# First attention of a four-layer kernel: the sum of queries and maxima moves from VectorE to TensorE and ScalarE

## The chip, the cores and the metric

One Trainium2 chip, one of its cores. The metric is the device time of the whole kernel in microseconds, smaller is better. TensorE (PE) multiplies, VectorE (DVE), ScalarE (ACT) and GpSimd (POOL) do the rest, and SyncE (SP) issues the transfers. PEld is the loading of TensorE's stationary operand, which overlaps its matmuls.

## The reference

Four layers follow one another: a cross attention with mean and deviation over 256 channels (the first attention, L0), and then three more attentions with their dense layers and MLPs (L1, L2, L3). The change is within L0 alone. There x and ctx have shape (8, 128, 256): 8 sequences, 128 channels, 256 positions; 16 heads of 8 channels each.

```python
q = jnp.einsum('oc,bct->bot', Wq, x) + bq[None, :, None]
k = jnp.einsum('oc,bct->bot', Wk, kv) + bk[None, :, None]
v = jnp.einsum('oc,bct->bot', Wv, kv) + bv[None, :, None]
...
attn = jnp.einsum('bhqd,bhdk->bhqk', q * scale, k)
attn = jnp.where(kv_mask[:, :, None, :], attn, -jnp.inf)
attn = jax.nn.softmax(attn, axis=-1)
mean = jnp.einsum('bhqk,bhkd->bhqd', attn, v)
ex2 = jnp.einsum('bhqk,bhkd->bhqd', attn, v * v)
std = jnp.sqrt(jax.nn.relu(ex2 - mean * mean))
...
out = (xn * std + mean) * mask.astype(x.dtype)
```

## The kernel before, in words

L0 is cut into 32 steps, four for each of the 8 sequences; a step handles four heads, and it has 4 units of work. The order in which all this is issued is written out by hand in `l0_order`: a list of ticks, one for each unit, to which every other piece is pinned. Every engine walks the same list and does its own share, so each engine works strictly in that order. `S` is the score matmul of a unit, `X` is its second score matmul, which is followed by the exponential.

One step s passes through these pieces:

- `pp` (tick 4s-7). TensorE picks the four heads out of the dense queries and keys with selection matrices (`sel`), which are the stationary operand: two matmuls of 256 columns for the queries (L895), two for the keys (L897) and one for the key mask (L898), all into one bank of PSUM. Queries and keys come as two parts each (`dqk`, a rounded value and the remainder), which is why there are two of each. ScalarE copies the bank to `qk` (L1183), adding a one in a row of each head through the bias `ones0`. SP then moves the keys into a block form (`kbd`) with four DMAs.
- `S` (ticks 4s to 4s+3). One matmul of 512 columns (L913) gives scores with queries down the partitions, into one of three banks. VectorE reduces each to the negated maximum of every row (L1552).
- `NL` (tick 4s+4). GpSimd writes those maxima into `NM` as a rounded part and a remainder (L1665, L1666).
- `P2` (tick 4s+6). TensorE transposes `NM` with two matmuls of 128 columns (L905) into a general bank, and VectorE adds the bank to the queries in `qk` and writes `qs2` (L1559). `qs2` thus holds the queries and, in rows of their own, the maxima to be subtracted.
- `X` (unit u at tick u+9, so the first of the step comes at tick 4s+9). Two matmuls of 256 columns (L922), keys stationary and `qs2` moving, give the scores with keys down the partitions, less the maximum; two banks. ScalarE takes the exponential of 128x512 into `pt` (L1188).
- `PV` (every second step, tick 4s+14 for odd s). 16 matmuls with 32-column weights, shown as 32, multiply by the values (L935); ScalarE copies the bank to `pv` (L1193). `N` transposes it (L945), and VectorE divides by the sums (L1566, L1571). `OUT`, once for each sequence, transposes again (L953), and ScalarE copies (L1197).

Once for each sequence there are also `dq` (dense queries and keys, L878 and L879; ScalarE's copies L1176 and L1177), `dl` (GpSimd splits these, L1651 and L1652), `dv` (values, L883, VectorE's L1542) and `vq`. Four times `nT` transposes the context (L627, ScalarE's L1005, VectorE's L1290). Twice the weights of the next layer are split (ScalarE L986, VectorE L1244). At the start VectorE also takes statistics of x (`xs`, L1305 and L1307).

In one tick the pieces of that tick come first, then `S(u)`, then `X(u-9)`. So around `P2(s)` TensorE issues P2(s), S(4s+6), X(4s-3), S(4s+7), X(4s-2), and so on, and ScalarE's list has the exponential of unit 4s-4, then P2's turn, then the exponential of unit 4s-3.

The general banks are two, taken in turn by all pieces that need one (`dq`, `dl`'s source, `dv`, `pp`, `P2`, `N`, `OUT`, `nT`); who fills one waits until the one before was read (`j_bank`, `freed_by`). An engine that has nothing to do with a bank skips it (`j_skip`).

Of the kernel before, what the change touches and what calls it, by code (L numbers as in the profile page):

```python
# [24 lines left out]
ACT = mybir.ActivationFunctionType  # L25
ALU = mybir.AluOpType
AX = mybir.AxisListType

P = 128
B = 8  # L30
D = 256
# [54 lines left out]
L0_STACKS = 4  # L86
# [248 lines left out]
def build(nc, x, ctx_in, mask_t, mask_s2, mask_s3, packs, cols, rows, l2rows, inds, ident_in, out):  # L335
    stack = ExitStack()
    with stack:
# [143 lines left out]
        def C(name, i=0):  # L481
            return col[:, COLS[name][0] + i:COLS[name][0] + i + 1]
# [102 lines left out]
        def _(pe):  # L585
# [276 lines left out]
            def l0():  # L862
                for e, i, *k in l0_order():
# [35 lines left out]
                    elif e == "P2":  # L899
                        if s == 0:  # L900
                            pe.wait_ge(ident_r, 1)
                        pe.wait_ge(Z["nl"], s + 1)
                        bank = j_bank()
                        for im in range(2):
                            last = nc.tensor.matmul(bank[:, im * P:(im + 1) * P], NM[:, s % 3, im, :], identR, start=True, stop=True)  # L905
                        j_full(last, (Z["s2"], s + 1))
                    elif e == "S":
                        if j == 0:
                            pe.wait_ge(kb_in[s % 2], 64 * (s // 2 + 1))
                        if i >= len(L0_S):  # L910
                            pe.wait_ge(Z["mx"], i - len(L0_S) + 1)
                        p, im = divmod(j, 2)
                        nc.tensor.matmul(ps[:, L0_S[i % len(L0_S)], :], qk[:, s % L0_STACKS, im * P:(im + 1) * P],  # L913
                                         kbd[s % L0_BLOCKS][:, 2 * p:2 * p + 2, :], start=True, stop=True).then_inc(Z["sm"], 1)
                    elif e == "X":
                        if j == 0:
                            pe.wait_ge(Z["s2"], s + 1)
                        if i >= len(L0_X):
                            pe.wait_ge(Z["ex"], i - len(L0_X) + 1)
                        bank = ps[:, L0_X[i % len(L0_X)], :]  # L920
                        for t in range(2):
                            last = nc.tensor.matmul(bank[:, t * D:(t + 1) * D], kbd[s % L0_BLOCKS][:, j, t * P:(t + 1) * P], qs2[:, s % 2, :],  # L922
                                                    start=True, stop=True)
                        last.then_inc(Z["xm"], 1)
                    elif e == "PV":
                        b = i // 2
                        pe.wait_ge(Z["ex"], 8 * i + 8)
                        if i % 2 == 0:
                            pe.wait_ge(Z["vals"], b + 1)
                        if i > 0:  # L930
                            pe.wait_ge(Z["pv"], i)
                        for s in (2 * i, 2 * i + 1):
                            for t in range(2):
                                for j in range(4):
                                    last = nc.tensor.matmul(ps[32 * j:32 * j + 32, L0_O, s % 2 * D:(s % 2 + 1) * D],  # L935
                                                            va[:, b % 2, t, 4 * j + s % 4, :],
                                                            pt[:, (4 * s + j) % L0_PTS, t * D:(t + 1) * D], start=t == 0, stop=t == 1)
                        last.then_inc(Z["pm"], 1)
                    elif e == "N":
                        pe.wait_ge(Z["pv"], i + 1)  # L940
                        if i == 0:
                            pe.wait_ge(d_in, 16 * 3)
                        bank = j_bank()
                        for k in range(4):
                            last = nc.tensor.transpose(bank[:, k * P:(k + 1) * P], pv[:, i % 2, k * P:(k + 1) * P], ident[:, :])  # L945
                        j_full(last, (Z["nat"], i + 1))
                    elif e == "OUT":
                        pe.wait_ge(Z["nat"], 2 * i + 2)
                        bank = j_bank()
                        for kind in range(2):  # L950
                            for im in range(2):
                                at = kind * D + im * P
                                last = nc.tensor.transpose(bank[:, at:at + P], nat[:, i % 2, im, kind, :], ident[:, :])  # L953
                        j_full(last, (Z["oeA"], i + 1))
# [11 lines left out]
        def _(act):  # L966
# [190 lines left out]
            def l0():  # L1157
                for e, i, *k in l0_order():
                    if e == "w":
                        take(i)  # L1160
                    elif e == "nT":
                        norm_step(e, i, k[0])
                    elif e in ("dv", "P2", "N"):
                        j_skip()
                    elif e == "fin":
                        act.wait_ge(l0var, 2 * i + 2)
                        nc.scalar.activation(ms[:, 1, 2 * i:2 * i + 2, :], ms[:, 1, 2 * i:2 * i + 2, :], ACT.Sqrt).then_inc(l0dev, 1)
                    elif e == "sq":
                        act.wait_ge(l0stat, 1)
                        act.wait_ge(eps_ok, 1)  # L1170
                        nc.scalar.activation(sd[:, 1, :], sd[:, 0, :], ACT.Sqrt, bias=eps[:, 0:1]).then_inc(l0sq, 1)
                    elif e == "dq":
                        bank = j_take()
                        if i > 0:
                            act.wait_ge(Z["dense"], i)
                        nc.scalar.activation(xqk[:, 0, :], bank[:, 0:D], ACT.Identity, bias=C("L0q"))  # L1176
                        nc.scalar.activation(xqk[:, 1, :], bank[:, D:2 * D], ACT.Identity, bias=C("L0k")).then_inc(Z["xq"], 1)  # L1177
                    elif e == "pp":
                        bank = j_take()
                        if i >= L0_STACKS:  # L1180
                            act.wait_ge(Z["s2"], i - L0_STACKS + 1)
                            act.wait_ge(Z["sm"], 4 * (i - L0_STACKS) + 4)
                        nc.scalar.activation(qk[:, i % L0_STACKS, :], bank, ACT.Identity, bias=C("ones0")).then_inc(Z["st"], 1)  # L1183
                    elif e == "X":
                        act.wait_ge(Z["xm"], i + 1)
                        if i >= L0_PTS:
                            act.wait_ge(Z["pm"], (i - L0_PTS) // 8 + 1)
                        nc.scalar.activation(pt[:, i % L0_PTS, :], ps[:, L0_X[i % len(L0_X)], :], ACT.Exp, scale=Q0_SCALE).then_inc(Z["ex"], 1)  # L1188
                    elif e == "PV":
                        act.wait_ge(Z["pm"], i + 1)  # L1190
                        if i >= 2:
                            act.wait_ge(Z["nat"], i - 1)
                        nc.scalar.copy(pv[:, i % 2, :], ps[:, L0_O, :]).then_inc(Z["pv"], 1)  # L1193
                    elif e == "OUT":
                        bank = j_take()
                        act.wait_ge(xn_done, i + 1)
                        nc.scalar.copy(ms[:, :, i, :], bank.rearrange("p (k n) -> p k n", k=2)).then_inc(Z["oeA"], 1)  # L1197
# [13 lines left out]
        def _(dve):  # L1211
# [9 lines left out]
            def j_take():  # L1221
                j = taken[0]
                taken[0] += 1
                dve.wait_ge(jm, j + 1)
                return ps[:, J_BANK + j % 2, :]
# [4 lines left out]
            def f32(ap):  # L1230
                return ap.bitcast(F32)
# [274 lines left out]
            def l0():  # L1506
                for e, i, *k in l0_order():
# [15 lines left out]
                    elif e == "fin":  # L1523
# [4 lines left out]
                        dve.wait_ge(l0mul, i + 1)  # L1528
                        link(nc.vector.tensor_tensor(X[:, two, :], X[:, two, :], ms[:, 0, two, :], ALU.add))
                        nc.vector.tensor_tensor(X[:, two, :], X[:, two, :], mt8[:, two, :], ALU.mult).then_inc(fin, 2)  # L1530
                    elif e in ("dq", "pp", "OUT"):
                        j_skip()
                    elif e == "dv":
                        bank = j_take()
# [12 lines left out]
                    elif e == "S":  # L1547
                        dve.wait_ge(Z["sm"], i + 1)
                        if j == 0 and s >= 3:
# [2 lines left out]
                        nc.vector.tensor_reduce(nm[:, s % 3, im, 2 * p:2 * p + 2],  # L1552
                                                ps[:, L0_S[i % len(L0_S)], :].rearrange("p (h n) -> p h n", h=2),
                                                AX.X, ALU.max, negate=True).then_inc(Z["mx"], 1)
                    elif e == "P2":
                        bank = j_take()
                        if i >= 2:
                            dve.wait_ge(Z["xm"], 4 * (i - 2) + 4)
                        nc.vector.tensor_tensor(qs2[:, i % 2, :], bank[:, 0:D], f32(qk[:, i % L0_STACKS, 0:D]), ALU.add).then_inc(Z["s2"], 1)  # L1559
                    elif e == "N":  # L1560
                        b = i // 2
                        bank = j_take().rearrange("p (g c) -> p g c", c=32)
# [26 lines left out]
        def _(pool):  # L1589
# [53 lines left out]
            def l0():  # L1643
                for e, i, *k in l0_order():
                    if e == "dl":
                        pool.wait_ge(Z["xq"], i + 1)
                        if i >= 2:
                            pool.wait_ge(Z["st"], 4 * (i - 1))
                        src = xqk.rearrange("p a n -> p (a n)")
                        hi, lo = dqk[:, i % 2, 0, :], dqk[:, i % 2, 1, :]  # L1650
                        link(nc.gpsimd.tensor_copy(hi, src))  # L1651
# [163 lines left out]
```

## Time and profile before

| | |
|---|---|
| median of 3 runs | 1260.13 us |
| the three runs | 1251.97, 1260.76, 1260.13 us |
| the profiled execution | 1252.72 us, with a span of 1250.9 us |
| granted clock of TensorE, mean of the span | 0.947 |
| busy in the span: PE, PEld, DVE, ACT, POOL | 1109.2, 960.1, 746.2, 723.7, 320.7 us |
| first P2 add and last P2 add on VectorE | 33.4 us and 187.0 us |

The span is the time from the first to the last instruction that the profiler recorded. L0's steps lie between about 24 and 196 us of it. The profiled execution is 7.4 us under the median; the three runs have two levels, near 1252 and near 1260 us.

### The profile page before, as it was taken

The numbers are of one execution on the slowest core, as the hardware profiler recorded it, in microseconds if no ns is written. First come the engines' busy times: TensorE is split into PE (matmuls) and PEld (weight loads), VectorE is DVE, ScalarE is ACT, GpSimd is POOL, SyncE is SP. The second block draws the span as 40 slices with busy tenths as digits, with TensorE's granted clock in tenths as the row PEclk, the third lists the DMA queues.
The fourth block names the chain that finished last, engine by engine and source line by source line (L and its number), as shares of the span: only waits on it lengthen the run. The fifth ranks groups of instructions, "written<-read, shape, count | busy, mean of one in ns | idle before, by whom it ended". The sixth has DMA issues, their size and how long they took to land. (4 is left out here: it accounts for less than half of the span.)

```text
span 1250.9 us, 23776 instructions
## 1 busy us (share of the span) xinstructions
PE 1109.2 (89%) x8224; PEld 960.1 (77%) x8224; DVE 746.2 (60%) x1761; ACT 723.7 (58%) x2096; POOL 320.7 (26%) x433
## 2 busy tenths in 40 slices
PE   3899995999978989999999899999998696899687
PEld 3677774667758879999998789999997695676486
DVE  4777774677776535555556735555555847455653
ACT  1577774777764356666665555666665423777531
POOL 5234344555430002111111122111111202332210
PEclk9899997999988999999999989999998897799899
DMA  6111101000002101111111011111101101000101
GB/s 197 25 29 53 34 23 34 2 2 1 1 31 81 43 26 43 43 43 43 43 64 43 1 43 43 43 43 43 43 35 35 51 2 34 2 2 1 34 1 35
DMA packets 20364, 43.65 MB, mean 35 GB/s; under 512 B 3347, under 2 KB 10773, under 8 KB 20246
## 3 DMA queue, kind: packets, MB, share of 16 engines
q1 hardware_dynamic: 20246, 42.12, 10.1%
q8 instruction: 68, 1.11, 0.4%
q14 instruction: 50, 0.41, 0.1%
HBM read 36.87 MB, written 1.05 MB: 30 GB/s over the span
## 5 line engine op out<-in xcount | busy, mean ns | idle before, releaser
L1601 POOL TENSOR_TENSOR pt<-pt,prec 128x256 f32<-128x256 f32 (+1 forms) x224 | 179.8, 803 | 669.2 <-DVE prec L1445 514.0
L604 PE MATMUL ps<-rs 128*128 128x256 f32 x480 | 147.2, 307 | 29.7 <-DVE rs L1480 19.6
L1109 ACT ACTIVATE pt<-ps,nmax 128x129 f32<-128x129 f32 x256 | 92.1, 366 | 96.7 <-DVE nmax L1437 95.9
L1244 DVE TENSOR_TENSOR rs<-wraw,rs 128x256 fp32r<-128x256 f32 (+2 forms) x108 | 69.2, 644 | 122.9 <-ACT rs L986 122.1
L605 PE MATMUL ps<-rs 128*128 128x256 f32 x480 | 139.3, 290 | 0.0
L606 PE MATMUL ps<-rs 128*128 128x256 f32 x480 | 139.3, 290 | 0.0
L1060 ACT ACTIVATE pt<-ps,nmax 128x256 f32<-128x256 f32 (+1 forms) x256 | 104.9, 421 | 48.0 <-DVE nmax L1383 30.0
L604 PE MATMUL ps<-ht,rs 128*128 128x256 f32 (+1 forms) x368 | 127.5, 346 | 1.0 <-ACT fs L1147 1.0
L604 PEld LDWEIGHTS ps<-rs 128*128 128x128 f32 x480 | 95.5, 199 | 36.0 <-DVE rs L1480 12.7
L605 PE MATMUL ps<-ht,rs 128*128 128x256 f32 (+1 forms) x368 | 121.2, 329 | 0.0
L606 PE MATMUL ps<-ht,rs 128*128 128x256 f32 (+1 forms) x368 | 120.9, 328 | 0.0
L1383 DVE TENSOR_REDUCE nmax<-ps 128x2 f32<-128x512 f32 (+1 forms) x96 | 66.2, 689 | 52.4 <-PE ps L715 43.3
L605 PEld LDWEIGHTS ps<-rs 128*128 128x128 f32 x480 | 95.7, 199 | 0.0
L606 PEld LDWEIGHTS ps<-rs 128*128 128x128 f32 x480 | 95.5, 199 | 0.0
L1147 ACT ACTIVATE fs<-ps,col 128x256 f32<-128x256 f32 x96 | 40.3, 471 | 93.9 <-PE ps L606 87.7
L1459 DVE SCALAR_TENSOR_TENSOR rs<-ps,col,rs 128x256 fp32r<-128x256 f32 x128 | 61.9, 484 | 46.5 <-ACT rs L1126 46.4
L604 PE MATMUL ps<-rs,ct 128*128 128x256 f32 x288 | 87.7, 305 | 1.0 <-DVE fs L1421 0.9
L1552 DVE TENSOR_REDUCE nm<-ps 128x2 f32<-128x512 f32 x128 | 81.9, 682 | 5.7 <-PE ps L913 5.6
L792 PEld LDWEIGHTS ps<-fs 128*128 128x128 f32 x512 | 76.6, 192 | 10.2
L605 PE MATMUL ps<-rs,ct 128*128 128x256 f32 x288 | 81.5, 283 | 0.0
L606 PE MATMUL ps<-rs,ct 128*128 128x256 f32 x288 | 81.4, 283 | 0.0
L1188 ACT ACTIVATE pt<-ps 128x512 f32<-128x512 f32 x128 | 73.2, 598 | 12.0 <-PE ps L922 10.2
(196 smaller groups left out, 3009.5 us busy)
## 6 DMA issues: line engine op xcount, KB each, us to landing
wraw<-in_packs SPq DMA_DIRECT2D x55, 512.0 KB, 3.4
bvr<-in_l2rows SPq DMA_DIRECT2D x16, 256.0 KB, 4.5
rs<-rs SPq DMA_DIRECT2D x80, 32.0 KB, 1.9
ht<-rs SPq DMA_DIRECT2D x48, 32.0 KB, 1.9
row<-in_rows SPq DMA_DIRECT2D x2, 640.0 KB, 4.8
out<-X SPq DMA_DIRECT2D x1, 1024.0 KB, 5.0
X<-in_x SPq DMA_DIRECT2D x1, 768.0 KB, 8.4
XH<-in_ctx SPq DMA_DIRECT2D x1, 768.0 KB, 10.2
```

The source lines that it names most:

```text
L604: nc.tensor.matmul(dst, w[0], m[1], start=start, stop=False)
L605: nc.tensor.matmul(dst, w[1], m[0], start=False, stop=False)
L606: return nc.tensor.matmul(dst, w[0], m[0], start=False, stop=stop)
L792: last = nc.tensor.matmul(ps[:, S_BANK + g % 2, b * D:b * D + P + 1], qT[:, hh % 3, 2 * b2 + b, :], kT[:, hh % 3, 2 * b2 + b, :], start=Tr ...
L1060: last = nc.scalar.activation(prob[:, i % 3, h * keys:(h + 1) * keys], ps[:, SCORE_BANKS[ph][i % len(SCORE_BANKS[ph])], h * keys:(h + 1) * ...
L1109: last = nc.scalar.activation(prob[:, g % 3, k * D:k * D + P + 1], ps[:, S_BANK + g % 2, k * D:k * D + P + 1], ACT.Exp, bias=nmax[:, g % 4 ...
L1188: nc.scalar.activation(pt[:, i % L0_PTS, :], ps[:, L0_X[i % len(L0_X)], :], ACT.Exp, scale=Q0_SCALE).then_inc(Z["ex"], 1)
L1244: last = nc.vector.tensor_tensor(dst[1], src, f32(dst[0]), ALU.subtract)
L1383: nc.vector.tensor_reduce(nmax[:, i % 4, 0:nh], ps[:, SCORE_BANKS[ph][i % len(SCORE_BANKS[ph])], :].rearrange("p (h n) -> p h n", h=nh), A ...
L1459: nc.vector.scalar_tensor_tensor(cc[1][:, hd, two, :], ps[:, O_BANK + g % 2, 0:D].rearrange("p (b n) -> p b n", b=2), C(f"L2bv{p // PAIRS ...
L1552: nc.vector.tensor_reduce(nm[:, s % 3, im, 2 * p:2 * p + 2], ps[:, L0_S[i % len(L0_S)], :].rearrange("p (h n) -> p h n", h=2), AX.X, ALU.m ...
L1601: nc.gpsimd.tensor_tensor(pr, pr, prec[:, u % 4, 0:nh].unsqueeze(2).broadcast_to([P, nh, keys]), ALU.mult)\
```

## The change

In `P2`, TensorE's two transposing matmuls become four in one accumulation group: after the two for the maxima, two more matmuls add the queries into the same bank columns, with the same selection matrices and the same dense queries as in `pp`. ScalarE then copies the bank to `qs2`, with the bias `ones0` that the copy of `pp` has, and waits for what VectorE waited for. VectorE skips the bank. Because `dqk` of a sequence is now read once more, later, by `P2`, the splitting of the dense queries and keys two sequences on (`dl`) waits for `P2`'s copy (`s2`) where it waited for that of `pp` (`st`).

```diff
                         bank = j_bank()
                         for im in range(2):
-                            last = nc.tensor.matmul(bank[:, im * P:(im + 1) * P], NM[:, s % 3, im, :], identR, start=True, stop=True)
+                            nc.tensor.matmul(bank[:, im * P:(im + 1) * P], NM[:, s % 3, im, :], identR, start=im == 0, stop=False,
+                                             skip_group_check=True)
+                        for p in range(2):
+                            last = nc.tensor.matmul(bank[:, 0:D], sel[:, 4 * m + p, :], dqk[:, b % 2, p, 0:D], start=False, stop=p == 1,
+                                                    skip_group_check=True)
                         j_full(last, (Z["s2"], s + 1))
...
-                    elif e in ("dv", "P2", "N"):
+                    elif e in ("dv", "N"):
                         j_skip()
...
+                    elif e == "P2":
+                        bank = j_take()
+                        if i >= 2:
+                            act.wait_ge(Z["xm"], 4 * (i - 2) + 4)
+                        nc.scalar.activation(qs2[:, i % 2, :], bank[:, 0:D], ACT.Identity, bias=C("ones0")).then_inc(Z["s2"], 1)
...
-                    elif e in ("dq", "pp", "OUT"):
+                    elif e in ("dq", "pp", "P2", "OUT"):
                         j_skip()
...
-                    elif e == "P2":
-                        bank = j_take()
-                        if i >= 2:
-                            dve.wait_ge(Z["xm"], 4 * (i - 2) + 4)
-                        nc.vector.tensor_tensor(qs2[:, i % 2, :], bank[:, 0:D], f32(qk[:, i % L0_STACKS, 0:D]), ALU.add).then_inc(Z["s2"], 1)
...
                         if i >= 2:
-                            pool.wait_ge(Z["st"], 4 * (i - 1))
+                            pool.wait_ge(Z["s2"], 4 * (i - 1))
```

## Rows read from the trace of the kernel before

**Rows 1.** Busy time by stretch of L0: engine busy (instructions), clock, DMA

```profile
24.00:40.00 16.00, 14.07 (x50) 11.26 (x50) 15.42 (x38) 5.29 (x9) 3.75 (x8) 0.79 0.13 31
...
60.00:80.00 20.00, 18.97 (x172) 14.93 (x174) 14.83 (x34) 15.08 (x28) 8.13 (x17) 1.00 0.13 32
...
120.00:140.00 20.00, 19.18 (x169) 15.12 (x172) 14.22 (x35) 14.90 (x28) 7.78 (x17) 1.00 0.20 55
```

**Rows 2.** Waits from 40 to 186 us: total us, times, longest

```profile
DVE rs L1559 <- PE ps L905: 31.2, 15, 4.4
...
PEld ps L922 <- ACT pt L1188: 5.1, 19, 0.6
...
PEld ps L953 <- DVE fs L1571: 4.1, 5, 0.9
...
PEld ps L913 <- DVE nm L1552: 2.4, 2, 1.2
```

**Rows 3.** Timeline, the `P2` of an odd step: start, length, idle before

```profile
92.68 0.30 PEld L905 LDWEIGHTS ps<-rs 128*128 128x128 f32 x2 [0.41 <-issue]
92.68 0.44 PE L905 MATMUL ps<-rs 128*128 128x128 f32 x2
...
92.82 0.59 ACT L1193 COPY fs<-ps 128x512 f32<-128x512 f32 x1 [1.06 <-PE ps L935]
92.89 0.19 PEld L913 LDWEIGHTS ps<-rs 128*128 128x128 f32 x1
...
93.16 0.42 DVE L1559 TENSOR_TENSOR rs<-ps,rs 128x256 fp32r<-128x256 f32 x1 [2.64 <-PE ps L905]
93.24 0.40 PE L922 MATMUL ps<-rs 128*128 128x256 f32 x2
...
93.50 1.28 DVE L1552 TENSOR_REDUCE nm<-ps 128x2 f32<-128x512 f32 x2
93.68 1.08 ACT L1188 ACTIVATE pt<-ps 128x512 f32<-128x512 f32 x2 [0.28 <-PE ps L922]
```

**Rows 4.** Timeline, weight loads of one `pp` after another

```profile
115.49 0.30 PEld L895 LDWEIGHTS ps<-rs,sel 128*128 128x128 f32 x2
...
115.73 0.31 PEld L897 LDWEIGHTS ps<-rs,sel 128*128 128x128 f32 x2
...
115.97 0.19 PEld L898 LDWEIGHTS ps<-ht,rs 128*128 128x128 f32 x1
```

**Rows 5.** Timeline, ScalarE's two copies of 128x256 in `dq`, and the `PV` ahead of them

```profile
111.56 1.45 PEld L935 LDWEIGHTS ps<-pt,fs 128*32 128x32 f32 x32 [0.33 <-ACT pt L1188]
...
111.67 0.47 ACT L1176 ACTIVATE fs<-ps,col 128x256 f32<-128x256 f32 x1 [0.17 <-PE ps L879]
112.04 0.47 ACT L1177 ACTIVATE fs<-ps,col 128x256 f32<-128x256 f32 x1
```

**Rows 6.** Timeline, the `P2` of an even step and ScalarE around it

```profile
116.41 0.69 ACT L1183 ACTIVATE rs<-ps,col 128x512 fp32r<-128x512 f32 x1
...
116.68 0.34 PE L905 MATMUL ps<-rs 128*128 128x128 f32 x2
...
116.99 2.37 ACT L1188 ACTIVATE pt<-ps 128x512 f32<-128x512 f32 x4
...
117.64 0.30 PEld L922 LDWEIGHTS ps<-rs 128*128 128x128 f32 x2 [0.19 <-ACT pt L1188]
```

**Rows 7.** Timeline, the stretch in which VectorE takes the statistics of x

```profile
42.10 0.42 DVE L1559 TENSOR_TENSOR rs<-ps,rs 128x256 fp32r<-128x256 f32 x1
42.44 1.28 DVE L1552 TENSOR_REDUCE nm<-ps 128x2 f32<-128x512 f32 x2
...
46.92 1.19 PE L878 MATMUL ps<-X,fs 128*128 128x256 f32 x2 [2.93 <-DVE fs L1542]
```

**Rows 8.** Timeline, after the last `P2`

```profile
187.02 0.42 DVE L1559 TENSOR_TENSOR rs<-ps,rs 128x256 fp32r<-128x256 f32 x1 [2.90 <-PE ps L905]
187.31 4.17 ACT L1188 ACTIVATE pt<-ps 128x512 f32<-128x512 f32 x7
```

## The prediction

> **What bounds the kernel now.** I read the busy times by stretch first, then the waits, then the timeline of single steps. All of the change lies in the first attention, from about 24 to 196 us of the span, so nothing outside it can answer except by being shifted. Between 60 and 160 us the work repeats every two sequences, at full granted clock, and TensorE is busy 19.0 to 19.2 us out of 20, VectorE about 14.5 and ScalarE about 15 [rows 1]. A busy share is not yet a bound, so the waits have to say who waits for whom. From 40 to 186 us VectorE stands idle 31.2 us just ahead of the instruction that is taken away, waiting for TensorE's P2, while TensorE waits for VectorE's maxima only 2.4 us and for its division (N, ahead of OUT) 4.1 us; for ScalarE's exponentials it waits 5.1 us in 19 places [rows 2]. So TensorE sets the pace with ScalarE close behind it, and VectorE follows.
>
> The timeline shows the same in one step. PV occupies TensorE, then P2, then S and X in turn. The VectorE add comes after 2.64 us of idleness, and the maxima after it at 93.50 [rows 3]. The first X that reads the sum is three ticks later. Only at the start is it otherwise: while VectorE takes the statistics of x it works without a gap, and TensorE waits 2.93 us for its L1542 [rows 7].
>
> **TensorE gets two matmuls of 256 columns in each of 32 P2.** They are of the shape of L895 in pp: same stationary matrices, same moving operand. In a pp the load of L895's pair starts at 115.49, that of L897's pair at 115.73, that of L898 at 115.97 [rows 4]: a pair costs 0.24 us of TensorE's time, weights included (the records of 0.40 us for a pair overlap their neighbours). P2's old pair goes on in 0.21 us (loads at 92.68 and 92.89, [rows 3]) and stays. Where TensorE works without a gap nothing hides the new 0.24 us, and everything behind P2 moves by it: 32 x 0.24 = 7.7 us if nothing hides any.
>
> **VectorE loses 32 adds.** One takes 0.42 us by its record, and the next instruction starts 0.34 us after it (93.16 to 93.50, 42.10 to 42.44) [rows 3, 7]: 32 x 0.34 = 10.9 us of VectorE's time. Where does it land on the path? For steps 0, 1 and 2 VectorE is without a gap and TensorE waits for it, so there 3 x 0.34 = 1.0 us is won, and TensorE's extra matmuls vanish in its wait of 2.93 us [rows 7]. From step 3 on it stood idle ahead of nearly every second add, for as long as 2.64 us or more, and what the absent add gives is more idleness. The maxima can begin a little earlier after P2 (they can't begin before S ends, which TensorE's extra time puts off), but the S that waits for them is three units on. I take nothing there. The bound on the other side: if all of VectorE's 4.1 + 2.4 us by which TensorE waits for it [rows 2] went, 6.5 us would be won.
>
> **ScalarE gets 32 copies of 128x256 from PSUM to fp32r.** No such copy with this output type stands alone in L0; the nearest is the dq copy with a bias column, 0.47 us by its record, and the next starts 0.37 us after it [rows 5]. I take 0.38 us of ScalarE's time (the record of 0.47 overlaps the next), 12.2 us in all. What of it shows depends on the place:
> - Odd steps (3, 5, ... 31, fifteen of them): P2 follows PV, and ScalarE is in the copy of PV, from 92.82 to some 93.40, as P2's bank fills. With the two new matmuls the bank is full at 92.68 + 0.44 + 0.24 = 93.36; the copy goes from 93.41 to 93.79. X ended at 93.64 and will end at 93.88, and the exponential started at 93.68, that is, it will start at 93.92 [rows 3]. The copy fits ahead of it, so only TensorE's 0.24 shows. 15 x 0.24 = 3.6 us.
> - Even steps (4, 6, ... 30, fourteen of them): P2 follows no PV, and ScalarE has no gap there in half of them: the pp copy at 116.41, then four exponentials in a row from 116.99, and TensorE's X waits 0.19 us for one [rows 6]. The copy goes in between, all four move by 0.38, and X with them: 0.38, of which TensorE's own 0.24 is a part, not an addition. In the other half OUT stands ahead, whose copy ends about when P2's bank fills, and the delay lies between 0.24 and 0.38 or a little more. I take 0.34: 14 x 0.34 = 4.8 us.
> - After the last P2 ScalarE does seven exponentials in a row and TensorE waits for them [rows 8]: 0.38 and not 0.24, another 0.1 us.
> Can this be won back by the end of a pair of steps? PV starts when the exponential of the last unit is done, after a wait of 0.33 us [rows 5], and that follows TensorE's pp and ScalarE's copy of it. The chain goes from TensorE to ScalarE and back, and neither has a gap in it in which a delay would be lost. Exceptions are the two places where TensorE waits up to 1.2 us for maxima, while weights are split [rows 2]: a few tenths.
>
> **The other waits.** ScalarE's copy waits for X of two steps back, which is long done. Behind it in ScalarE's list stands the exponential of unit 4s-3, whose delay is priced above. The next general bank that needs P2's bank is the second one after it, over 0.4 us off. X(4s) needs the sum three ticks after P2, some 3 us later; the sum comes at most 0.4 us later than before. GpSimd's dl now waits for s2 of a P2 two ticks earlier in the list; GpSimd does a NL in between that needs maxima taken later still. Queued behind dl are vr, xn and the next NL. I cost this at nothing; if it did show, it would delay pp of a new sequence, seven times. No DMA is added or moved, and the four key DMAs hang on pp's copy.
>
> **The sum.** -1.0 + 3.6 + 4.8 + 0.1 = +7.5 us. On the profiled execution, 1252.7 us (span 1250.9), that is 1260.2. The runs have two levels, 1252 and 1260.1 to 1260.8, and the profile is on the lower. I put the sum on the median, 1260.1: 1267.6 us, +0.6%. A measurement of this kernel can hardly tell less than 1% (12.6 us) from no change.
>
> **Rivals.**
> 1. The new matmuls and the copy hide: TensorE has gaps for them, and the time stays. For it: the weight loads are busy only 15.0 us in 20 [rows 1], and TensorE does wait 5.1 us for exponentials. Against it: the matmuls' own records leave hardly a microsecond in 20. It would give -1.0 to +2 us, some 1260 us. The Trainium skill (Perfetto Trace Analysis, Identifying the Most-Contended Engine) speaks for this rival: the busy share of matmuls says little about how close TensorE is to its limit, that of LDWEIGHTS should be read instead. By that reading a quarter of the stretch would be free, the added work would cost next to nothing, and the forecast would be about 1260. The rows of the timeline decide for me: a chain without gaps delays all that follows, whatever the share. Chance 0.18.
> 2. The other side, faster: VectorE's add is what holds the chain. It would do so if maxima, NL and the next P2 followed each other without slack, so that each 0.34 us off VectorE brings the next P2 forward, and outweighs TensorE's 0.24. It decides from the point where TensorE's P2 waits for GpSimd's NL. The most it gives is 10.9 us less, 1249; with TensorE's share taken off, 1257. Against it: 31.2 us of VectorE idle at that very add [rows 2]. Chance 0.05.
> 3. ScalarE becomes the bound: its delay of 0.38 adds to TensorE's 0.24 in every step instead of overlapping with it, as P2's bank fills while ScalarE is free, and the exponential then waits for the copy. 29 x 0.62 = 18, less 1.0: +17 us, 1277. For it: ScalarE goes from 15.0 to 15.0 + 4 x 0.38 = 16.5 us in 20, and it is on the chain at each PV. Against it: in odd steps the copy of PV hides the wait. Chance 0.12.
>
> **How the numbers follow.** The forecast has 0.65. Its own bounds: all extra at TensorE's 0.24 and the wins at the start, 29 x 0.24 - 1 = +6; or 0.38 in every step with TensorE's wait unchanged, 29 x 0.38 = +11; partly hidden at the two splits and at dl, +4. So 1264 to 1271. The two levels of the runs add several microseconds below. The range reaches down through rival 1 and takes a part of rival 3: 1257 to 1274. Under 1% less than now (1247.5) only the extreme of rival 2 lies: 0.02. Over 1% more (1272.7) rival 3 and an edge of the forecast: 0.14. The rest, 0.84, is within 1%.
>
> **What would show it.** P2 with four matmuls, S's weights loaded 0.45 us after P2's first load and not 0.21; from one PV to the next 0.5 to 0.6 us more for two steps, where 31 steps now take 153.6 us from the first add to the last (33.4 to 187.0), 9.9 us for two; the last exponential of L0 some 7 to 8 us later, and all behind it shifted by as much. VectorE's idle time before L1552 should grow. X's wait for L1188 should grow at the even steps. The prediction is wrong if the distance from PV to PV grows by 0.1 or less (rival 1), shrinks (rival 2) or grows by over 1 us (rival 3).

## The result, and the profile after

Over 20 runs each, the changed kernel took 1264.32 us in the median (1259.45 to 1268.84) and the kernel before 1260.14 us (1251.97 to 1263.97). The ratio is 1.0042, 95% interval 1.0023 to 1.0061: between 2.9 and 7.7 us more, 5.3 in the middle. The medians are 4.2 us apart. The forecast was +7.5 us, 1267.6 in a range of 1257 to 1274.

The profiled execution of the changed kernel took 1265.84 us with a span of 1264.1, which is 13.2 us more span than before. Only some 5 us of that had come up by the last P2 of the first attention; the rest lies behind it, with a different granted clock, so the two traces have to be compared piece by piece.

First the same P2 as in [rows 3], one sequence earlier, in the timeline of the changed kernel:

```profile
72.60 0.30 PEld L905 LDWEIGHTS ps<-rs 128*128 128x128 f32 x2 [0.41 <-issue]
72.60 0.44 PE L905 MATMUL ps<-rs 128*128 128x128 f32 x2
72.74 0.59 ACT L1202 COPY fs<-ps 128x512 f32<-128x512 f32 x1 [1.05 <-PE ps L939]
72.82 0.30 PEld L908 LDWEIGHTS ps<-rs,sel 128*128 128x128 f32 x2
...
73.05 0.19 PEld L917 LDWEIGHTS ps<-ht,rs 128*128 128x128 f32 x1
...
73.37 0.47 ACT L1192 ACTIVATE rs<-ps,col 128x256 fp32r<-128x256 f32 x1
73.40 0.40 PE L926 MATMUL ps<-rs 128*128 128x256 f32 x2
...
73.60 1.29 DVE L1561 TENSOR_REDUCE nm<-ps 128x2 f32<-128x512 f32 x2 [3.16 <-PE ps L917]
...
73.83 1.08 ACT L1197 ACTIVATE pt<-ps 128x512 f32<-128x512 f32 x2
```

L905 to L917 is 0.45 us where it was 0.21: the new pair L908 costs 0.23 to 0.24. ScalarE's new copy (L1192) stands between PV's copy and the exponential. X ends at 73.80 and the exponential starts at 73.83, as soon after X as before; the copy fits. VectorE's maxima begin after 3.16 us of idleness where the add began after 2.64.

The distance from one such P2 to another is a clean measure, since from 66 us to the P2 of step 31 the granted clock is 1.00 in both. From the P2 of step 7 to that of step 31 (24 steps) it was 71.93 to 186.54 us, 114.61 us; now it is 72.60 to 191.59, 118.99 us: **+4.38 us**. The first row is that of the kernel before, the second of the changed one, in the timeline of each:

```profile
186.54 0.30 PEld L905 LDWEIGHTS ps<-rs 128*128 128x128 f32 x2 [0.41 <-issue]
```

```profile
191.59 0.30 PEld L905 LDWEIGHTS ps<-rs 128*128 128x128 f32 x2 [0.41 <-issue]
...
192.36 0.47 ACT L1192 ACTIVATE rs<-ps,col 128x256 fp32r<-128x256 f32 x1
...
192.73 4.16 ACT L1197 ACTIVATE pt<-ps 128x512 f32<-128x512 f32 x7
...
196.94 3.38 PE L939 MATMUL ps<-pt,fs 128*32 128x256 f32 x32 [0.69 <-ACT pt L1197]
```

From the last P2 to the last PV it is 5.35 us after 4.99 (the last PV began at 191.53 before), +0.36. The first of the seven exponentials starts 1.14 us after the P2 where it had started 0.77 after it (186.54 and 187.31). That last PV then took 3.38 us where it had taken 1.93. The busy times by stretch of the changed kernel show the clock there: in the first row (187 to 196 us) TensorE has the full 2.4 GHz; in the second, in that PV, the granted clock is 0.51, its lower level. In the kernel before it was 1.00 in that PV.

```profile
187.00:196.00 9.00, 8.03 (x67) 5.41 (x66) 2.57 (x8) 7.20 (x14) 3.77 (x6) 1.00 0.01 2
197.00:200.00 3.00, 3.00 (x32) 1.33 (x32) 0.00 (x0) 0.00 (x0) 0.00 (x0) 0.51 0.00 0
```

From there to 1035 us of the span the delay stays at 6.0 to 6.9 us. In the last layer it grows to 12.2: the same ScalarE instruction L1147 (now L1151) stands at 1035.41 and 1041.77, and again at 1209.10 and 1221.32. The edit touches nothing there. The granted clock does differ, between 1040 and 1120 us of the span before (first row) and about the same work after (second):

```profile
1040.00:1120.00 80.00, 63.13 (x433) 50.27 (x432) 46.42 (x106) 49.20 (x187) 28.23 (x26) 0.83 0.04 14
```

```profile
1046.00:1131.00 85.00, 69.17 (x439) 55.16 (x437) 45.98 (x112) 50.19 (x190) 28.93 (x26) 0.78 0.04 13
```

The waits of the changed kernel, 65 to 186 us (total, times, longest), against the same stretch of the kernel before, which follows:

```profile
DVE nm L1561 <- PE ps L917: 28.8, 23, 3.2
...
PEld ps L926 <- ACT pt L1197: 3.2, 10, 0.3
...
PEld ps L917 <- DVE nm L1561: 1.9, 2, 0.9
```

```profile
PEld ps L922 <- ACT pt L1188: 3.7, 15, 0.4
...
PEld ps L913 <- DVE nm L1552: 2.4, 2, 1.2
...
PEld ps L895 <- POOL rs L1652: 0.8, 3, 0.3
```

The later kernel does some 5 us less of its work in the same stretch, so the totals are better taken between the P2 of step 7 and that of step 31 of each: there TensorE waited 3.4 us for exponentials before and 3.3 after. That wait did not grow. Its two waits for maxima became shorter by 0.25 us each (2.4 to 1.9 us), and three waits for GpSimd's split of the dense queries (L895 on L1652) are gone.

### The profile page after: what moved, and what is told of

Its sections match the earlier page's. It is cut to its first block and busy times, and to the rows that moved or that the text cites. A ratio compares the mean times of both kernels' runs of the same rounds, so it can differ in the third digit from the quotient of the medians.

```text
span 1264.1 us, 23904 instructions
## 1 busy us (share of the span) xinstructions
PE 1121.4 (89%) x8288; PEld 972.5 (77%) x8288; DVE 737.8 (58%) x1729; ACT 736.3 (58%) x2128; POOL 320.6 (25%) x433
## 5 line engine op out<-in xcount | busy, mean ns | idle before, releaser
L604 PE MATMUL ps<-rs 128*128 128x256 f32 x480 | 149.1, 311 | 29.2 <-DVE rs L1489 19.1
L605 PE MATMUL ps<-rs 128*128 128x256 f32 x480 | 141.0, 294 | 0.0
L606 PE MATMUL ps<-rs 128*128 128x256 f32 x480 | 140.9, 294 | 0.0
L604 PEld LDWEIGHTS ps<-rs 128*128 128x128 f32 x480 | 97.3, 203 | 35.5 <-DVE rs L1489 12.7
L605 PEld LDWEIGHTS ps<-rs 128*128 128x128 f32 x480 | 97.6, 203 | 0.0
L606 PEld LDWEIGHTS ps<-rs 128*128 128x128 f32 x480 | 97.3, 203 | 0.0
L1151 ACT ACTIVATE fs<-ps,col 128x256 f32<-128x256 f32 x96 | 40.3, 471 | 94.8 <-PE ps L606 89.2
L814 PE MATMUL ps<-pt,fs 128*128 128x128 f32 x512 | 79.0, 277 | 0.0
```

The costliest lines, as they stand in the source:

```text
L604: nc.tensor.matmul(dst, w[0], m[1], start=start, stop=False)
L605: nc.tensor.matmul(dst, w[1], m[0], start=False, stop=False)
L606: return nc.tensor.matmul(dst, w[0], m[0], start=False, stop=stop)
L814: last = nc.tensor.matmul(ps[:, O_BANK + g % 2, b * P:(b + 1) * P], v2[:, p % 2, 2 * b2 + b, hd, :], probT[:, g % 3, b * P:(b + 1) * P], s ...
```

## Experiments

Theory T, formed on this profile: the cost is TensorE's own 0.24 us per P2, nothing else. That another wait swallows it in some steps was added after the first eight runs (e1 to e8). Rival S: ScalarE's copy is the cost and the matmuls hide. Rival V: VectorE's absent add wins something back. The noise of the whole time is several microseconds, most of it outside the first attention, so every kernel was also read from its own trace: the distance from the P2 of step 7 to that of step 31, at granted clock 1.00 in all of them.

| kernel | P2 of steps 7 and 31, us | distance, us | against before | ratio of whole times, 95% interval |
|---|---|---|---|---|
| before | 71.93, 186.54 | 114.61 | | |
| changed | 72.60, 191.59 | 118.99 | +4.38 | 1.0042 (1.0023 to 1.0061) |
| e1_matmuls_alone | 76.67, 196.17 | 119.51 | +4.90 | 1.0027 (0.9998 to 1.0056) |
| e2_copy_alone | 71.44, 187.17 | 115.73 | +1.12 | 1.0012 (0.9986 to 1.0038) |
| e3_add_cut | 74.05, 188.35 | 114.30 | -0.31 | 0.9988 (0.9966 to 1.0011) |
| e4_sum_vector_copy | 74.81, 194.68 | 119.86 | +5.25 | 1.0008 (0.9988 to 1.0027) |
| e5_copy_twice | 73.93, 198.45 | 124.51 | +9.90 | 1.0073 (1.0047 to 1.0099) |
| e6_matmuls_twice | 72.02, 195.99 | 123.98 | +9.37 | 1.0057 (1.0039 to 1.0075) |
| e7_split_waits | 74.68, 189.27 | 114.58 | -0.03 | 0.9984 (0.9964 to 1.0005) |
| e8_pp_vector | 76.17, 196.33 | 120.16 | +5.55 | 1.0077 (1.0057 to 1.0097) |
| e9_split_first_before | 73.79, 186.98 | 113.20 | -1.41 | 0.999 (0.9962 to 1.0018) |
| e10_split_first_after | 72.92, 191.46 | 118.53 | +3.92 | 1.0039 (1.0011 to 1.0068) |

**The matmuls alone.** On the kernel before:

```diff
                         for im in range(2):
                             last = nc.tensor.matmul(bank[:, im * P:(im + 1) * P], NM[:, s % 3, im, :], identR, start=True, stop=True)
+                        for p in range(2):
+                            last = nc.tensor.matmul(bank[:, D:2 * D], sel[:, 4 * m + p, :], dqk[:, b % 2, p, 0:D], start=p == 0, stop=p == 1)
                         j_full(last, (Z["s2"], s + 1))
...
-                            pool.wait_ge(Z["st"], 4 * (i - 1))
+                            pool.wait_ge(Z["s2"], 4 * (i - 1))
```

> The kernel before, with the two selection matmuls added to P2, but into bank columns that nobody reads (the result stays that of before), and with the changed wait of dl; VectorE adds as before, ScalarE has no copy. Theory T (TensorE's own time is the whole cost): the distance from the exponentials near 57 us to those near 180 us grows by 0.24 us a step, 24 steps, +6 us against before, as with the whole change, and the time is that of the changed kernel within 1.5 us plus the 1 us that VectorE won at the start. Rival S (ScalarE's copy is the cost, the matmuls hide): the distance stays within 1 us of before. Rival V (the absent add wins something back in the steady part): the distance grows by more than with the whole change, by 8 us or more.

+4.90 us in the steady part: the matmuls alone cost as much as the whole change there, a little more. S falls. T expected +6 and got 4.9, since five steps of 24 hardly grow (they grow by 0.01 to 0.08 us, all others by 0.21 to 0.29). The 0.5 us over the changed kernel lies in these five steps, 0.09 to 0.11 in each, and 0.10 in step 29. The add of VectorE is present here and absent there, and it has the right size (the add cut, below), but ScalarE's copy differs too, so this pair alone doesn't show that it is the add.

**The copy alone.** On the changed kernel:

```diff
                         for im in range(2):
-                            nc.tensor.matmul(bank[:, im * P:(im + 1) * P], NM[:, s % 3, im, :], identR, start=im == 0, stop=False,
-                                             skip_group_check=True)
-                        for p in range(2):
-                            last = nc.tensor.matmul(bank[:, 0:D], sel[:, 4 * m + p, :], dqk[:, b % 2, p, 0:D], start=False, stop=p == 1,
-                                                    skip_group_check=True)
+                            last = nc.tensor.matmul(bank[:, im * P:(im + 1) * P], NM[:, s % 3, im, :], identR, start=True, stop=True)
```

> The changed kernel without the two selection matmuls: qs2 holds the maxima but not the queries, so the queries are left out of the exponentials' scores. ScalarE copies, VectorE does not add. Theory T: the steady part is as long as before, within 1 us, and the whole time within 2 us of before. Rival S: it is as long as in the changed kernel, +6 us. Rival V: it is shorter than before by 1 us or more. My prediction's term for even steps (0.34 where TensorE alone gives 0.24) asks for at least 14 x 0.1 = 1.4 us, and up to 7 x 0.38 = 2.7 us if a delay of ScalarE passes on whole where it has no gap.

+1.12 us, beside the +6 that S wanted. By single steps it is +0.11 to +0.18 from the P2 that follows an OUT to the next, 0 to 0.06 from most of those that follow a PV, and -0.03 to -0.07 in five of the even steps without OUT; the sixth of these has +0.27, and the last PV step -0.05. Where OUT stands ahead, the two timelines of step 6 read (this kernel, then the changed one; ScalarE's OUT copy is L1202 here and L1206 there, its P2 copy L1188 and L1192, the exponential L1193 and L1197):

```profile
65.27 0.59 ACT L1202 COPY fs<-ps 128x512 f32<-128x512 f32 x1
...
65.57 0.39 PE L922 MATMUL ps<-rs 128*128 128x256 f32 x2
...
65.74 0.50 ACT L1188 ACTIVATE rs<-ps,col 128x256 fp32r<-128x256 f32 x1
...
66.11 0.62 ACT L1193 ACTIVATE pt<-ps 128x512 f32<-128x512 f32 x1
```

```profile
66.32 0.59 ACT L1206 COPY fs<-ps 128x512 f32<-128x512 f32 x1
...
66.83 0.47 ACT L1192 ACTIVATE rs<-ps,col 128x256 fp32r<-128x256 f32 x1
66.86 0.39 PE L926 MATMUL ps<-rs 128*128 128x256 f32 x2
...
67.29 1.79 ACT L1197 ACTIVATE pt<-ps 128x512 f32<-128x512 f32 x3
```

With the matmuls absent, X ends at 65.96 and the exponential starts 0.15 us later, behind the copy; with them it starts 0.04 us after X's end (67.25), as it did before (66.58 and 66.62). In the later steps with OUT ahead it starts 1.00 us after P2 in the kernel before, 1.16 with the copy alone, 1.24 in the changed kernel. The two delays meet at one handover, and here the larger one counts.

After the last P2 they don't meet so. From it to the last PV it is 4.99 us before, 5.23 with the matmuls alone, 5.21 with the copy alone and 5.35 with both, more than either. No S stands between the X any more, and the exponential had started as early as 0.77 us after P2. The copy, right behind that of PV, starts 0.62 us after P2 in this kernel. In the changed one ScalarE waits for the bank, which is full later, and the copy starts at 0.77; the exponential stands behind it. Part of TensorE's delay and the copy add up, which is what the prediction's third rival had for every step.

**The add cut.** On the kernel before (most of the sum is left out, and GpSimd clears `qs2` once at the start):

```diff
-                        nc.vector.tensor_tensor(qs2[:, i % 2, :], bank[:, 0:D], f32(qk[:, i % L0_STACKS, 0:D]), ALU.add).then_inc(Z["s2"], 1)
+                        nc.vector.tensor_tensor(qs2[:, i % 2, 0:8], bank[:, 0:8], f32(qk[:, i % L0_STACKS, 0:8]), ALU.add).then_inc(Z["s2"], 1)
```

> The kernel before with VectorE's add in P2 cut to 8 of 256 columns, so most of the sum is left out and the rest of qs2 stays zero. It shows what VectorE's time is worth. Theory T: nothing in the steady part (within 0.5 us), some 1 us at the start. Rival V: 0.1 us a step or more, over 2.5 us in the steady part.

-0.31 us in 24 steps, 0.05 to 0.07 in each of the same five and in step 29. V is right in sign and too small to matter. The start can be read apart from the clock, since VectorE works there without a gap that TensorE makes: from the start of its sum of the mask (the `TENSOR_REDUCE` of uint8) to the end of the second `dv` it takes 21.23 us before, 21.23 with the matmuls alone, 20.24 in the changed kernel and 20.24 with the copy alone. The absent adds win 0.99 us there. TensorE's first matmul behind it (L878) waits for that `dv` in both, 2.9 us before and 2.4 in the changed kernel, so the win is on its path.

**The sum with VectorE's copy.** On the changed kernel, the copy of P2 goes back to VectorE as `nc.vector.tensor_scalar(qs2[:, i % 2, :], bank[:, 0:D], C("ones0"), None, ALU.add)`, and ScalarE skips the bank.

> The changed kernel with its copy given back to VectorE: TensorE forms the sum, VectorE copies it with the bias, ScalarE is as before. Theory T: as the changed kernel in the steady part, +6 us against before, within 1 us. Rival S: as before there, within 1 us.

+5.25 us, as T has it. ScalarE has nothing of the change here and the cost is all there.

**Doses.** On the changed kernel, ScalarE's copy twice (the first into a spare tile), and two more selection matmuls:

```diff
+                        nc.scalar.activation(spare, bank[:, 0:D], ACT.Identity, bias=C("ones0")).then_inc(Z["sc"], 1)
                         nc.scalar.activation(qs2[:, i % 2, :], bank[:, 0:D], ACT.Identity, bias=C("ones0")).then_inc(Z["s2"], 1)
```

> The changed kernel with ScalarE's copy done twice, the first into a spare tile. It asks how much room ScalarE has left. Theory T: ScalarE has little room, since it hands over to the exponential with hardly a gap after the first copy; a second copy shows with up to its 0.37 us in the odd steps and in the even ones, 24 x 0.37 = +9 us against the changed kernel in the steady part, at least +5. If ScalarE had room for the first copy with much to spare (the copy of no consequence at all), under +2 us.

```diff
+                        for p in range(2):
+                            last = nc.tensor.matmul(bank[:, D:2 * D], sel[:, 4 * m + p, :], dqk[:, b % 2, p, 0:D], start=False, stop=p == 1,
+                                                    skip_group_check=True)
```

> The changed kernel with two more selection matmuls in each P2, into bank columns that nobody reads. Theory T: another 0.24 us a step, 24 steps, +6 us in the steady part against the changed kernel, some +7 on the whole. Rival S: under +2 us, since matmuls hide.

A second copy adds 5.5 us to the changed kernel's steady part, though the first had cost nothing beside the matmuls. The timeline of its P2 of step 7 shows the exponential (L1199) at 75.43, while X (L927) ended at 75.13: it now waits 0.30 us, behind the second copy. In that step most of the wait is made up again before the next P2; by single steps the second copy adds 0.06 to 0.09 us in seven of them, of which this is one, nothing in step 29, 0.26 to 0.31 in ten and 0.33 to 0.39 in six, the five free ones among them.

```profile
74.70 0.48 ACT L1193 ACTIVATE rs<-ps,col 128x256 fp32r<-128x256 f32 x1
74.73 0.40 PE L927 MATMUL ps<-rs 128*128 128x256 f32 x2
...
75.07 0.47 ACT L1194 ACTIVATE rs<-ps,col 128x256 fp32r<-128x256 f32 x1
...
75.43 1.09 ACT L1199 ACTIVATE pt<-ps 128x512 f32<-128x512 f32 x2
```

Two more matmuls add 4.99 us, that is again some 0.24 in the steps that grow, 0.17 to 0.19 in steps 16, 20 and 24, and nothing in 8 and 12. TensorE's price is paid from the first matmul on; ScalarE's is small for the first copy (+1.12 us alone) and 5.5 us for the second, though in a third of the steps even the second finds room.

**The wait of dl alone.**

```diff
-                            pool.wait_ge(Z["st"], 4 * (i - 1))
+                            pool.wait_ge(Z["s2"], 4 * (i - 1))
```

> The kernel before with only the wait of GpSimd's dl changed from pp's copy to P2's sum. The prediction costs this at nothing: within 0.5 us of before in the steady part. If it is a cost, it delays pp of each new sequence, and the change of 0.25 us a step is made of fewer and larger delays.

-0.03 us, and no single step differs by more than 0.02. It costs nothing, as forecast.

**What makes some steps free.** The five steps are those from the P2 of step 8, 12, 16, 20 and 24 to the next. In the kernel before, TensorE stands idle there in three of them, ahead of the pp of a new sequence, for GpSimd's dl. This is its timeline:

```profile
118.22 0.50 PE L922 MATMUL ps<-rs 128*128 128x256 f32 x2
...
118.78 0.30 PEld L895 LDWEIGHTS ps<-rs,sel 128*128 128x128 f32 x2 [0.26 <-POOL rs L1652]
```

GpSimd does vq before dl in that tick. Two kernels have vq a tick later, one on either side of the change:

```diff
-            put(16 * b + 4, "vq", b)
+            put(16 * b + 5, "vq", b)
```

> The kernel before with one piece of GpSimd's list moved: the squares of the values (vq) come a tick later, behind the split of the dense queries and keys (dl). In one step out of four the changed kernel is no slower than before; the theory is that TensorE's pp waits there for dl (0.26 us idle ahead of L895) and the two new matmuls vanish in that wait. If so, without that wait each of these six steps is some 0.25 us shorter between the P2 of step 7 and that of step 31: -1.5 us against before. If not, no difference there.

> The changed kernel with the same piece moved. If the wait for dl hid the matmuls, they now show in every step: against the kernel before with the same move, 24 x 0.24 = +5.8 us, and in the steps that showed nothing up to 0.38, since ScalarE's copy stands there between other work without a gap, so +5.8 to +6.6 us; against the changed kernel itself under 0.5 us less. If something else made those steps free, +4.4 us as before.

Without the change this wins 1.41 us in the steady part (expected 1.5), 0.20 to 0.35 in each of the five steps, and L895 has no idle time left on GpSimd. With the change it wins only 0.46, and in the three steps that had the wait (16, 20, 24) the matmuls now cost 0.27, 0.25 and 0.26 us, between the two kernels. In the other two (8 and 12) they still cost nothing. There VectorE splits the next layer's weights, and TensorE waits for its maxima, 1.1 us with vq moved and 0.9 with the change as well in the longest: 0.25 us less in each, which is the matmuls' time. For these two steps the cause is read from the waits alone; no run takes that wait away. Nor is it shown why moving vq wins 0.20 us in each of them, where no wait for dl stood; the wait for maxima gets only 0.1 us shorter. So between these two kernels it is 5.33 us, not the 5.8 or more that I expected of them: 22 steps grow and two don't.

The even steps without OUT side by side, us by which the way to the next P2 grew:

| from the P2 of step | 8 | 12 | 16 | 20 | 24 | 28 |
|---|---|---|---|---|---|---|
| changed, against before | -0.07 | -0.01 | -0.02 | -0.04 | -0.08 | 0.27 |
| matmuls alone, against before | 0.04 | 0.08 | 0.06 | 0.05 | 0.01 | 0.25 |
| copy alone, against before | -0.04 | -0.05 | -0.04 | -0.03 | -0.07 | 0.27 |
| both with vq moved | -0.03 | 0.01 | 0.27 | 0.25 | 0.26 | 0.26 |

Where nothing swallows it, the cost is 0.25 to 0.27 us, and it is so for the copy alone too (step 28). ScalarE's 0.37 never comes through whole. The trace shows where the rest went: in the kernel before, the four exponentials of [rows 6] start 0.58, 0.61 and 0.58 us apart, in the changed one (step 16) the copy stands between the first two, which are then 0.83 apart, and the next follows after 0.48. So ScalarE had about 0.1 us of room between one exponential and the next, which a row of merged records without a gap doesn't show.

**What the profile seemed to offer.** ScalarE's copy of pp stands just ahead of the last exponential before PV, and VectorE idles. On the kernel before, `pp`'s copy was given to VectorE as `nc.vector.tensor_scalar(qk[:, i % L0_STACKS, :], bank, C("ones0"), None, ALU.add)`, with the waits that ScalarE had.

> Not the change but what the profile points to: the kernel before with pp's copy (128x512, 0.69 us on ScalarE, just ahead of the last exponential that PV waits for) moved to VectorE, which idles 31 us ahead of its add. If ScalarE's copy ahead of PV is on the chain, each pair of steps loses up to 0.58 us of 9.9, and 16 pairs give up to -9 us. If VectorE gets there later than ScalarE (its list has maxima of 0.64 us each ahead of it), the keys' transfers and the exponentials come later: 0 to +10 us.

+5.55 us and a ratio of 1.0077: no win, but the other of the two outcomes. The way from an odd step's P2 to the next got longer by up to 0.87 us. Its timeline shows TensorE's P2 waiting for the bank that pp had filled, since VectorE's copy (L1554) stands behind the division (L1571) and a maximum:

```profile
90.02 0.62 DVE L1571 TENSOR_TENSOR fs<-ps,rcp 128x64 f32<-128x64 f32 x4
...
90.55 0.68 DVE L1546 TENSOR_REDUCE nm<-ps 128x2 f32<-128x512 f32 x1
...
91.15 0.74 DVE L1554 TENSOR_SCALAR rs<-ps,col 128x512 fp32r<-128x512 f32 x1
...
92.03 0.41 PE L905 MATMUL ps<-rs 128*128 128x128 f32 x2 [0.63 <-DVE rs L1554]
```

Of all twelve kernels the fastest in the steady part is the one before with vq moved (113.20 us). Its whole time, 0.999 with 0.9962 to 1.0018, is not to be told from before.

## Why the prediction was right

The sign and the place were right, and so was the mechanism but for the even steps; the size was 2 to 3 us too large (7.5 against 5.3 by the whole times and 4.7 by the trace). That the time fell into the range says little: 1257 to 1274 holds the kernel before, too. What bears the mechanism out is the steady part.

- **TensorE, 0.24 us for each P2.** Measured 0.24: 0.45 us from L905 to L917 after 0.21, and the twelve ways from an odd step's P2 to the next grew by 2.91 us together, 0.24 each, with 3.6 us forecast for fifteen.
- **VectorE's 1.0 us at the start, nothing after.** Measured 0.99 at the start, and 0.3 in the steady part by the add cut, 0.5 by the matmuls alone against the changed kernel.
- **ScalarE in the odd steps: fits ahead of the exponential.** It does (73.83, X's end 73.80).
- **ScalarE in the even steps, 0.34 us: this term was mis-sized.** The twelve even ones between the P2 of steps 8 and 31 grew by 1.47 us, 0.12 each. Two things were wrong in it. Where OUT stands ahead, I let the sum rise over TensorE's 0.24 toward ScalarE's 0.38, and the copy alone costs only 0.11 to 0.18 there, which the 0.24 covers. Where it doesn't, I read the four exponentials without a gap as a chain that passes 0.38 on [rows 6]. It passes on 0.25 to 0.27 (step 28, and 16, 20 and 24 with vq moved), and in five of the six steps even that was lost a little further, where TensorE waited for GpSimd's dl or for maxima. I had named dl and the two splits, but only as a bound of the range (+4); [rows 2] has no row for dl's wait, since three waits of 0.26 to 0.29 us stand low in that view.
- **After the last P2, 0.38 us.** Measured 0.36, but not because ScalarE's copy shows whole: alone it costs 0.22 there, and the matmuls alone 0.24. The number is right by luck.
- **The new wait of dl, nothing.** Measured -0.03.
- **The sum.** By the trace: -1.0 at the start, 0.7 for steps 3 to 5, whose P2 lie in stretches of changing clock and were not read singly (an estimate, 3 x 0.24), 0.23 from the P2 of step 6 to that of step 7, 4.38 and 0.36. That is +4.7, within the 2.9 to 7.7 of the whole times. In the prediction's bounds, +11 for 0.38 in every step leaves out the 1.0 us won at the start; with it the bound is +10.

Of the rivals, "it hides" had five steps in 24. The Trainium skill (Perfetto Trace Analysis, Identifying the Most-Contended Engine) has the LDWEIGHTS share, 15 us in 20 here, as one of two measures of TensorE's headroom. That is a statement on the distance from the limit, and read as the price of one more matmul it fails here: matmuls added at that share cost their time in 19 of 24 steps, and a second pair again. ScalarE as the bound (+17) would have needed the delays to add in every step; they did so in part after the last P2 alone. VectorE as the chain had 0.05 us or a little more in six steps.

Two signs that I had named came out otherwise. X's wait for the exponentials did not grow (3.4 us before, 3.3 after, between the same two P2). And from one odd P2 to the next, where I had 0.5 to 0.6 us more for two steps, it was 0.4 to 0.5 in seven pairs and 0.2 in the five that hold a free step, 0.36 in the mean.

What stays open is the whole time. The summed copy on VectorE is +5.25 us in the steady part and has no win at the start, yet its whole time is only 1 us above before (-1.5 to +3.4). A second pair of matmuls costs 4.99 us more in the steady part, and its whole time is some 2 us above the changed kernel's (1.0057 against 1.0042). The matmuls alone are 0.5 us above the changed kernel in the steady part and lack its 1 us at the start, and their whole time is some 2 us below it (1.0027). So the whole times don't confirm the 4.7 us of the trace more closely than their own intervals. The stretches after the first attention differ between executions by several microseconds with the granted clock, as in 6 us of the profiled difference here, and whether a change in the first attention shifts these was not tried.

## What to carry to other kernels

When work moves from an idle engine to two busy ones, price it where it lands: the engine without gaps pays for all of it, and the gain on the idle one is nearly all more idle time. Of two delays that run side by side to the same handover take the larger; where one starts only when the other ends, they add, in part at least. Look some microseconds further along the list for a wait on a third engine that swallows both. And before a row of instructions without idle time is called a chain, compare the distance of their starts with the shortest at which the engine has started them elsewhere. Where whole times scatter by more than the effect, measure between two marks in the trace at the same granted clock; hundredths of a microsecond become readable there.

## What the runs showed of the hardware

The same instructions in the same order took different times where the granted clock differed. The last PV of the first attention, 32 recorded matmuls, took 1.93 us at granted clock 1.00 (the kernel before, timeline below) and 3.38 us at 0.51 in the changed one, after the same 0.69 us of TensorE's idleness. The change is not what decides it: of the twelve kernels this PV took 3.3 to 3.5 us in four, the copy alone (3.48) among them, and 1.93 in the other eight, the second pair of matmuls among them.

```profile
191.53 1.93 PE L935 MATMUL ps<-pt,fs 128*32 128x256 f32 x32 [0.69 <-ACT pt L1188]
```

In the steady steps, by contrast, all at granted clock 1.00, each of the 24 took the same time within 0.02 us in the kernel before and in the one with the wait of dl alone.
